# A third pair of weight buffers for the steps, and the product into the state in split parts

## The chip, the cores and the metric

The kernel is written in Bass for one Trainium2 chip and runs on one of its NeuronCores. A core has five engines with queues of their own: TensorE (PE in the profile, with its weight loads as PEld), VectorE (DVE), ScalarE (ACT), GpSimd (POOL) and SyncE (SP), which here only starts transfers. They are ordered by semaphores alone, and each works through its queue in the order of the program. The metric is the device time of one execution in microseconds (us), the median of several runs.

## The reference

One layer of a state-space model on 1,024 tokens of width 512, with a small feed-forward beside it:

```python
xn = layernorm(x)
zxbcdt = xn @ in_proj_w.T                  # gate 8192, x 8192, B 1024, C 1024, dt 128
xBC = silu(causal_conv4(xBC) + conv_b)     # x: 128 heads x 64; B, C: 8 groups x 128
dt = softplus(dt + dt_bias); Adt = -exp(A_log) * dt
# in chunks: y = (C B^T * decay) (dt x)  +  C state * decay  +  D x
#            state = decay * state + B^T (decay * dt x)
y = y * silu(gate)
y = y * rsqrt(mean(y*y over each group of 1024) + eps) * norm_w
attn = y @ out_proj_w.T
# feed-forward: in each block of 32 of the 1,792 inner units only the one with the
# largest value of xn @ c1.T @ c2.T takes part
out = x + attn + (relu(xn @ w1.T) * chosen) @ w2t
```

All inputs and outputs are float32.

## The kernel before, in words

**Split products.** Where a product of float32 numbers is done in F32R, the quicker and coarser matmul form, each operand is kept as a high part (a copy rounded into F32R) and a low part (the number less its high part), and three matmuls, high by high, high by low and low by high, add up in PSUM. ScalarE makes the high part and GpSimd the low part. Products in plain F32 need no parts.

**The steps (`prologue`).** The feed-forward runs in STEPS = 28 steps, 14 slices of 128 inner units for each half of the tokens. Step n has an `inward` product (L764, twelve matmuls of 512 columns: three for each of four slices of the width), a selection mask that VectorE makes in `pick` and TensorE turns in `turn` (L780), the masked hidden units `hm` (`hidden_units`, L595), and an `outward` product (L793, twelve matmuls). Each product takes a weight tile of 128x512 from DRAM, called an item. Item 2n-1 is that of `inward(n)` (`item1`), item 2n+2 that of `outward(n)` (`item2`). An item is loaded by SP into one of AHEAD = 3 raw buffers `wxs` (L298), and `high(i)` on ScalarE (L445) and `low(i)` on GpSimd (L324) split it into one of two pairs `wxp[:, i % 2]`. So the high part of item i waits until the product that used item i-2 is done. TensorE's order is `gate(n+2)`, `inward(n+1)`, `turn(n+1)`, `outward(n)`. In step n ScalarE and GpSimd make the parts of the hidden units (`high_hidden` L462, `low_hidden` L334), then those of item 2n+2, then those of item 2n+3. In steps 12 to 19 the output weights of the first group pass through one tile `stage` as well: SP loads it (L311), ScalarE scales it (L523) and makes its high part (L525), GpSimd makes the low part (L413), SP stores both (L307, L308), and then loads the next. SP's queue holds, in turn, the load of an even item 2n+4, these stores, the load of the odd item 2n+5, and the next load of `stage`. At the end `high_tile` and `low_tile` (L450, L328) split the first two weight tiles of the scan, once the steps' products have freed the two pairs.

**The scan (`scan`).** For each half of the tokens and each of 8 groups (16 units), 18 weight tiles are projected onto 512 tokens (`project`, L1147): 8 x tiles, B and C, which are convolved (VectorE, `convolve`, L1626) and go through Silu into `xT`, and 8 z tiles, which go through Silu into `gT`. A unit has 4 cells of 128 tokens, so there are 64 cells; cell q does the scan of its tokens, while the tiles of the next unit are projected in between, 4 or 5 in a cell. The last unit has none. TensorE's order in cell q is: two tiles, the products within the chunk (`diagonal`, L1205), exponents of the decay (`segment`, L1212), a tile, the product out of the state (`from_state`, L1167), a tile, `segment`, the gram product (`gram`, L1236 and L1237), the output projection of cell q (`project_out`: high by high L1260, high by low weights L1246, low by high L1267; in the first cell of a unit L1267 comes before L1246), `square_sum` (L1276), a fifth tile if there is one, the product into the state (`into_state`, L1180: two plain F32 matmuls of 512 columns, for 56 of the 64 cells), and `turn_x` (L1192), transposes for the cell after the next.

Around it, on VectorE: `scale_x` writes `xdt` (L1711) and `xdec` (L1714), `add_state` (L1662) and `scale_state` (L1644) keep the state S, `take_gram` writes `gb` (L1721), `add_diagonal` and `gate` write y over the gate values `gT` (L1678, L1702), `sum_tiles` adds the squares of the eight tiles of y (L1737), reading with a step of 128 elements, `add_out` adds to `acc` (L1750). On ScalarE: `leave_bank` takes a projected tile out of PSUM (`tap` L1383, or `gate` L1391) and makes the high part of the tile after the next (L1376), `high_y` makes the high part of y (L1441), `square` its squares (L1434), `exp_a` and `exp_b` the decays (L1414, L1418). On GpSimd: the low part of each tile (L1526), `low_y` the low part of y (`yl`, L1557), `join` (L1550) and `rnorm` (L1574).

## Time and profile before

| what | value |
|---|---|
| runs | 1936.75, 1937.0 and 1935.7 us, median 1936.75 us |
| the profiled execution | 1943.26 us, its span 1941.5 us |
| mean granted TensorE clock in it | 0.988 of full speed |
| PE, matmuls | 1866.8 us busy, 96% of the span |
| PEld, weight loads | 1466.4 us, 76% |
| DVE | 1456.4 us, 75% |
| ACT | 1171.3 us, 60% |
| POOL | 956.3 us, 49% |
| DMA | 264.6 MB, mean 136 GB/s |

The steps with what precedes them last until about 263 us, the scan fills the rest. A row of the order of time gives the start, the duration, the engine, the line, the operation with the tiles written and read, and how many records are merged in it; in brackets, how long the engine was idle before it, and what released it. Records of TensorE overlap their neighbours, so that its pace is read from start to start. A plain F32 matmul leaves two records.

### The profile page before, as it was taken

Reading aid. Unit: us, or ns where it says so; the run is one execution under the profiler, and the core shown is the slowest. Engines: PE = TensorE matmul, PEld = TensorE weight load, DVE = VectorE, ACT = ScalarE, POOL = GpSimd, SP = SyncE. Lnnn points to the kernel's source line nnn. Section 1 sums busy time; section 2 is a strip of 40 time slices with the busy share of each in tenths; the row PEclk is TensorE's granted clock in tenths of the full one; section 3 lists DMA queues with packets and bytes.
Section 4 is the critical chain, followed back from the end, with each engine's and each line's share of the span. In section 5 each row is a group of like instructions: output and inputs, shape, how many; then the busy total and the mean of one; then the engine's idle time right before and its main releaser. Section 6 shows DMA issues by size and latency. Waiting matters only on the chain.

```text
span 1941.5 us, 29126 instructions
## 1 busy us (share of the span) xinstructions
PE 1866.8 (96%) x10310; PEld 1466.4 (76%) x10310; DVE 1456.4 (75%) x1713; ACT 1171.3 (60%) x1910; POOL 956.3 (49%) x704
## 2 busy tenths in 40 slices
PE   6897899999999999999999999999999999999987
PEld 5675667777777777777777777878787878787865
DVE  7976645878787877878786878686877787777766
ACT  4334346767777676767676556566665666565643
POOL 4765753545555455555454444444444444444333
PEclk9999999999999999999999999999999999999998
DMA  3324463445464646464647353333424252424231
GB/s 98 110 86 145 121 220 93 128 159 182 134 207 133 219 136 221 125 209 127 212 134 239 86 166 116 111 113 94 147 77 156 83 161 82 156 72 155 70 122 44
DMA packets 123981, 264.60 MB, mean 136 GB/s; under 512 B 18496, under 2 KB 25408, under 8 KB 123584
## 3 DMA queue, kind: packets, MB, share of 16 engines
q1 hardware_dynamic: 89120, 161.55, 26.6%
q10 hardware_dynamic: 34720, 101.20, 16.4%
q8 instruction: 85, 1.39, 0.3%
q14 instruction: 56, 0.46, 0.1%
HBM read 216.82 MB, written 45.88 MB: 135 GB/s over the span
## 4 chain that ended last, share of the span: by engine, by line
PE 79%; DMA 6%; POOL 5%; DVE 3%; issue 3%; ACT 3%; ACTq 1%; SPq 0%; DVEq 0%; POOLq 0%
PE bank L1147 38%; PE bank L1205 5%; PE bank L1246 5%; PE bank L1267 5%; PE bank L1260 5%; PE bank L1180 5%; PE bank L1167 4%; DMA wosl<-wlo_scratch 3%; PE bank L1212 3%; PE bank L793 3%; PE bank L1192 3%; POOL wxp L324 2%; DMA wlo_scratch<-stage 1%; POOL hmp L334 1%; PE bank L764 1%
## 5 line engine op out<-in xcount | busy, mean ns | idle before, releaser
L1147 PE MATMUL bank<-xnp,wxp 128*128 128x512 f32 x3432 | 863.3, 404 | 8.3 <-POOL wxp L1526 3.6
L1147 PEld LDWEIGHTS bank<-xnp,wxp 128*128 128x128 f32 x3432 | 635.6, 189 | 160.1 <-POOL wxp L1526 11.4
L1526 POOL TENSOR_TENSOR wxp<-wxs,wxp 128x512 fp32r<-128x512 f32 x286 | 382.1, 1339 | 530.7 <-ACT wxp L1376 530.0
L1626 DVE SCALAR_TENSOR_TENSOR conv<-bank,cws,conv 128x509 f32<-128x509 f32 (+2 forms) x480 | 358.0, 746 | 11.3
L1383 ACT ACTIVATE conv<-bank,cbs,cws 128x512 f32<-128x512 f32 x160 | 124.1, 776 | 281.5 <-PE bank L1147 258.1
L1557 POOL TENSOR_TENSOR yl<-gT,yh 128x1024 fp32r<-128x1024 f32 x63 | 153.6, 2438 | 216.3 <-ACT yh L1441 216.3
L1729 DVE SCALAR_TENSOR_TENSOR M<-M,gb 128x1024 f32<-128x1024 f32 x128 | 174.1, 1361 | 7.5 <-DVE gb L1721 0.5
L1376 ACT ACTIVATE wxp<-wxs 128x512 fp32r<-128x512 f32 x286 | 178.1, 623 | 0.0
L1427 ACT ACTIVATE ya<-xT,dch 128x128 f32<-128x128 f32 x512 | 156.2, 392 | 0.0
L1418 ACT ACTIVATE M<-bank 128x1024 f32<-128x1024 f32 x64 | 65.6, 1024 | 133.4 <-PE bank L1212 133.4
L1260 PE MATMUL bank<-wosh,yh 128*128 128x512 f32 x512 | 136.2, 408 | 5.3 <-issue 5.0
L1550 POOL TENSOR_TENSOR ya<-ya,ecs 128x1024 f32<-128x1024 f32 x56 | 134.0, 2392 | 8.5 <-ACT ya L1427 8.5
L1205 PEld LDWEIGHTS bank<-M,xdt 128*64 128x64 f32 x2048 | 113.0, 139 | 27.8 <-issue 25.8
L1205 PE MATMUL bank<-M,xdt 128*64 128x128 f32 x2048 | 128.6, 279 | 5.4 <-DVE acc L1750 3.5
L1246 PE MATMUL bank<-wosl,yh 128*128 128x512 f32 x512 | 132.7, 400 | 0.8 <-DMA wosl<-wlo_scratch 0.7
L1737 DVE TENSOR_REDUCE ys<-xdt 128x128 f32<-128x1024 f32 x64 | 129.4, 2022 | 1.6 <-ACT xdt L1434 1.6
L1267 PE MATMUL bank<-wosh,yl 128*128 128x512 f32 x512 | 130.0, 396 | 0.2 <-POOL yl L1557 0.2
L793 PE MATMUL bank<-wxp,hmp 128*128 128x512 f32 x336 | 96.9, 443 | 32.9 <-POOL wxp L324 30.7
L1672 DVE TENSOR_TENSOR ecs<-bank,ecs 128x1024 f32<-128x1024 f32 x56 | 68.6, 1225 | 76.4 <-PE bank L1167 63.4
L1391 ACT ACTIVATE gT<-bank 128x512 f32<-128x512 f32 x128 | 76.5, 598 | 70.0 <-PE bank L1147 69.3
L1246 PEld LDWEIGHTS bank<-wosl,yh 128*128 128x128 f32 x512 | 96.7, 190 | 26.2 <-DMA wosl<-wlo_scratch 3.2
L1267 PEld LDWEIGHTS bank<-wosh,yl 128*128 128x128 f32 x512 | 96.0, 188 | 24.1 <-POOL yl L1557 0.9
(179 smaller groups left out, 2840.9 us busy)
## 6 DMA issues: line engine op xcount, KB each, us to landing
wxs<-wp SPq DMA_DIRECT2D x288, 256.0 KB, 2.8
wosh<-whi_scratch ACTq DMA_DIRECT2D x64, 512.0 KB, 6.0
wosl<-wlo_scratch ACTq DMA_DIRECT2D x64, 512.0 KB, 11.1
ecs<-ecs_scratch ACTq DMA_DIRECT2D x112, 256.0 KB, 4.5
stage<-wout SPq DMA_DIRECT2D x64, 256.0 KB, 2.9
whi_scratch<-stagh SPq DMA_DIRECT2D x64, 256.0 KB, 2.0
wlo_scratch<-stage SPq DMA_DIRECT2D x64, 256.0 KB, 2.3
wxs<-w SPq DMA_DIRECT2D x56, 256.0 KB, 2.8
```

The costliest lines, as they stand in the source:

```text
L793: last = pe.matmul(total(half * CH + c), hmp[:, n % 2, a, c * P:(c + 1) * P], flat[b], start=f == 0 and a + b == 0, stop=f == FT - 1 and a ...
L1147: last = pe.matmul(bank(k), wxp[:, k % 2, a, kk, :], xnp[:, b, kk, :], start=kk == 0 and a + b == 0, stop=kk == KT - 1 and a == 1)
L1205: last = pe.matmul(Y[part, h // 2 * P:(h // 2 + 1) * P], xdt[:, q % 2, h * HD:(h + 1) * HD], M[:, h, :], start=True, stop=True)
L1246: last = pe.matmul(y_out, yh[:, t, :], wosl[:, t, :], start=False, stop=c == 0 and t == XT - 1)
L1260: pe.matmul(y_out, yh[:, t, :], wosh[:, t, :], start=t == 0, stop=False)
L1267: last = pe.matmul(y_out, yl[:, t, :], wosh[:, t, :], start=False, stop=c > 0 and t == XT - 1)
L1376: act.activation(wxp[:, k % 2, 0], wxs[:, k % AHEAD], ACT.Copy).then_inc(w_hi, 1)
L1427: last = act.activation(ya[:, t, :], xT[u % 2][:, 2 + t, tokens(q)], ACT.Copy, scale=dch[:, g, t:t + 1])
L1526: pool.tensor_tensor(wxp[:, k % 2, 1], wxs[:, k % AHEAD], wxp[:, k % 2, 0], ALU.subtract).then_inc(w_lo, 1)
L1557: pool.tensor_tensor(yl[:], gT[u % 2][:, :, tokens(q)], yh[:], ALU.subtract).then_inc(y_lo, 1)
L1626: last = dve.scalar_tensor_tensor(out=conv[:, n % CB, back:], in0=bank(k)[:, 0:TH - back], scalar=cws[:, g, j, i:i + 1], in1=conv[:, n % C ...
L1729: last = dve.scalar_tensor_tensor(out=M[:, hs], in0=M[:, hs], scalar=1.0, in1=bc(gb[:, 0, :], 1, [P, HG // 2, P]), op0=ALU.min, op1=ALU.mult)
```

## The change

In the steps, split items get buffers of their own, `wfp`, in RING = 3 pairs, and `wxp` is left to the scan. The high part of item i waits for the product that used item i-3. `high(2)` and `low(2)` are done before the first step, and in step n the parts of items 2n+3 and 2n+4 are made after those of the hidden units, in place of 2n+2 and 2n+3. The first two tiles of the scan are split in the last two steps.

In the scan, `into_state` becomes six F32R matmuls in place of two in F32. Its operands get parts: ScalarE copies `xdec` into `xdech` (`high_x`) and `gb[:, 1]` into `gbh` (`high_b`), VectorE subtracts for `xdecl` (`low_x`), GpSimd for `gbl` (`low_b`). A low part lies at the address of what it is taken from (`twice`). The low part of y is in the same way written over `gT`, no longer into a tile `yl`, so that `low_y` waits for the Square of the same cell (`y_sq`) and not for the output projection before. The squares are written with the tile's number innermost, so that the reduction reads neighbours, and their sum lies in the first 128 columns of the same buffer. `high_x(q+1)` stands behind the departure of the first tile of cell q, `high_b(q+1)` behind `exp_b(q+1)`, `low_x(q+1)` behind `gate(q)`, `low_b(q+1)` behind `low_y(q)`.

```diff
--- before
+++ after
@@ -58,6 +58,7 @@
 AHEAD = 3
+RING = 3
...
@@ -321,7 +323,8 @@
                 pool.wait_ge(s_hi, i + 1)
-                pool.tensor_tensor(wxp[:, i % 2, 1], wxs[:, i % AHEAD], wxp[:, i % 2, 0], ALU.subtract).then_inc(s_lo, 1)
+                pool.tensor_tensor(wfp[:, i % RING, 1], wxs[:, i % AHEAD], wfp[:, i % RING, 0],
+                                   ALU.subtract).then_inc(s_lo, 1)
...
@@ -395,14 +399,12 @@
             for n in range(STEPS):
-                if n < STEPS - 1:
-                    low_hidden(n)
-                    low(item2(n))
-                else:
-                    low(item2(n))
-                    low_hidden(n)
-                if n + 2 < STEPS:
-                    low(item1(n + 2))
+                low_hidden(n)
+                for i in (2 * n + 3, 2 * n + 4):
+                    if i < 2 * STEPS:
+                        low(i)
+                if n >= STEPS - 2:
+                    low_tile(n - STEPS + 2)
                 mask_part(n)
...
@@ -505,17 +505,17 @@
             copy_mask(0)
+            high(2)
             for n in range(STEPS):
-                if n < STEPS - 1:
-                    high_hidden(n)
-                    high(item2(n))
-                else:
-                    high(item2(n))
-                    high_hidden(n)
+                high_hidden(n)
+                if 2 * n + 3 < 2 * STEPS:
+                    high(2 * n + 3)
                 if n + 1 < STEPS:
                     copy_mask(n + 1)
-                if n + 2 < STEPS:
-                    high(item1(n + 2))
+                if 2 * n + 4 < 2 * STEPS:
+                    high(2 * n + 4)
+                if n >= STEPS - 2:
+                    high_tile(n - STEPS + 2)
                 if OUTW <= n < OUTW + XT:
@@ -562,8 +562,6 @@
                                       tabs[:, half].rearrange("p g a c h -> p g (a c h)")).then_inc(d_saved, 16)
-            for k in range(2):
-                high_tile(k)
...
@@ -787,7 +785,7 @@
                     pe.wait_ge(s_add, CH)
-                flat = [wxp[:, i % 2, b].rearrange("p k c -> p (k c)") for b in range(2)]
+                flat = [wfp[:, i % RING, b].rearrange("p k c -> p (k c)") for b in range(2)]
                 for c in range(CH):
@@ -907,9 +905,15 @@
+    def twice(name, shape):
+
+        with ExitStack() as once:
+            full = sb(once, name, shape)
+        return full, sb(ctx, name + "l", shape, F32R)
+
     with ExitStack() as ctx:
         xT = [sb(ctx, f"xT{p}", [P, WT, TH]) for p in range(2)]
-        gT = [sb(ctx, f"gT{p}", [P, XT, TH]) for p in range(2)]
+        gT, gTl = zip(*(twice(f"gT{p}", [P, XT, TH]) for p in range(2)))
         wosh = sb(ctx, "wosh", [P, XT, HID], F32R)
@@ -919,13 +923,13 @@
         xdt = sb(ctx, "xdt", [P, 2, GC])
-        xdec = sb(ctx, "xdec", [P, GC])
+        xdec, xdecl = twice("xdec", [P, GC])
+        xdech = sb(ctx, "xdech", [P, GC], F32R)
         ecs = sb(ctx, "ecs", [P, XT, P])
         yh = sb(ctx, "yh", [P, XT, P], F32R)
-        yl = sb(ctx, "yl", [P, XT, P], F32R)
         ya = sb(ctx, "ya", [P, XT, P])
-        ys = sb(ctx, "ys", [P, P])
-        gb = sb(ctx, "gb", [P, 2, P])
+        gb, gbl = twice("gb", [P, 2, P])
+        gbh = sb(ctx, "gbh", [P, P], F32R)
         one = sb(ctx, "one", [P, 1])
...
@@ -999,7 +1004,15 @@
-            return xdt[:, q % 2].rearrange("p (t i) -> p t i", t=XT)
+            return xdt[:, q % 2].rearrange("p (i t) -> p t i", t=XT)
+
+        def square_sums(q):
+
+            return xdt[:, q % 2, 0:P]
+
+        def gated_low(q):
+
+            return gTl[q // CH % 2][:, :, tokens(q)]
@@ -1173,12 +1186,14 @@
                     return
-                pe.wait_ge(x_dec, done(q + 1))
-                pe.wait_ge(g_cp, done(q + 1))
+                pe.wait_ge(x_lo, done(q + 1))
+                pe.wait_ge(b_lo, done(q + 1))
                 pe.wait_ge(e_b, done(q + 1))
                 for b in range(2):
-                    last = pe.matmul(X[:, b * 512:(b + 1) * 512], gb[:, 1, :], xdec[:, b * 512:(b + 1) * 512],
-                                     start=True, stop=True)
+                    part = slice(b * 512, (b + 1) * 512)
+                    pe.matmul(X[:, part], gbh[:], xdech[:, part], start=True, stop=False)
+                    pe.matmul(X[:, part], gbh[:], xdecl[:, part], start=False, stop=False)
+                    last = pe.matmul(X[:, part], gbl[:, 1], xdech[:, part], start=False, stop=True)
                 last.then_inc(st_mm, 1)
...
@@ -1444,6 +1459,20 @@
                         act.activation(yh[:, part], gT[u % 2][:, part, tokens(q)], ACT.Copy).then_inc(y_hi, 1)
+
+            def high_x(q):
+                if dead(q):
+                    act.sem_inc(x_hi, 1)
+                    return
+                act.wait_ge(x_dec, done(q + 1))
+                act.activation(xdech[:], xdec[:], ACT.Copy).then_inc(x_hi, 1)
+
+            def high_b(q):
+                if dead(q):
+                    act.sem_inc(b_hi, 1)
+                    return
+                act.wait_ge(g_cp, done(q + 1))
+                act.activation(gbh[:], gb[:, 1], ACT.Copy).then_inc(b_hi, 1)
...
@@ -1477,6 +1509,8 @@
                     load_ecs(q + 1)
+                if more:
+                    high_x(q + 1)
                 if fill:
@@ -1494,6 +1528,7 @@
                     exp_b(q + 1)
+                    high_b(q + 1)
                 load_row(q + 2)
...
@@ -1551,16 +1586,23 @@
                 u, _, _, _ = place(q)
-                pool.wait_ge(o_mm, done(q))
+                pool.wait_ge(y_sq, done(q + 1))
                 if q + 1 < CELLS:
                     pool.wait_ge(y_hi, done(q + 1))
-                    pool.tensor_tensor(yl[:], gT[u % 2][:, :, tokens(q)], yh[:], ALU.subtract).then_inc(y_lo, 1)
+                    pool.tensor_tensor(gated_low(q), gT[u % 2][:, :, tokens(q)], yh[:], ALU.subtract).then_inc(y_lo, 1)
                 else:
                     for n in range(2):
                         part = slice(n * XT // 2, (n + 1) * XT // 2)
                         pool.wait_ge(y_hi, done(q + 1 + n))
-                        pool.tensor_tensor(yl[:, part], gT[u % 2][:, part, tokens(q)], yh[:, part],
+                        pool.tensor_tensor(gated_low(q)[:, part], gT[u % 2][:, part, tokens(q)], yh[:, part],
                                            ALU.subtract).then_inc(y_lo, 1)
+
+            def low_b(q):
+                if dead(q):
+                    pool.sem_inc(b_lo, 1)
+                    return
+                pool.wait_ge(b_hi, done(q + 1))
+                pool.tensor_tensor(gbl[:, 1], gb[:, 1], gbh[:], ALU.subtract).then_inc(b_lo, 1)
...
@@ -1588,6 +1631,8 @@
                 low_y(q)
+                if q + 1 < CELLS:
+                    low_b(q + 1)
                 for k in tiles_of(q)[3 if closes(q) else 2:4]:
...
@@ -1714,6 +1760,13 @@
+            def low_x(q):
+                if dead(q):
+                    dve.sem_inc(x_lo, 1)
+                    return
+                dve.wait_ge(x_hi, done(q + 1))
+                dve.tensor_tensor(xdecl[:], xdec[:], xdech[:], ALU.subtract).then_inc(x_lo, 1)
+
             def take_gram(q):
@@ -1734,7 +1787,7 @@
                 dve.wait_ge(q_mm, done(q))
-                dve.tensor_reduce(ys[:], squares(q).rearrange("p t i -> p i t"), AX.X, ALU.add).then_inc(y_s, 1)
+                dve.tensor_reduce(square_sums(q), squares(q).rearrange("p t i -> p i t"), AX.X, ALU.add).then_inc(y_s, 1)
...
@@ -1767,6 +1822,8 @@
                 gate(q)
+                if more:
+                    low_x(q + 1)
                 for k in ks[2:3]:
```

## Rows read from the trace of the kernel before

**Rows 1.** Table by stage: us, busy times of five engines, clock, DMA share, GB/s.
```profile
70.00:84.00 14.00, 13.10 (x67) 9.76 (x67) 13.72 (x16) 4.38 (x8) 12.12 (x10) 1.00 0.31 92
182.00:196.00 14.00, 10.20 (x44) 7.90 (x43) 8.46 (x15) 7.74 (x14) 5.27 (x5) 0.76 0.47 151
600.00:1000.00 400.00, 398.12 (x2201) 311.11 (x2200) 309.80 (x350) 281.96 (x463) 212.66 (x164) 1.00 0.53 171
```

**Rows 2.** List of waits in the steps (40 to 275 us): total us, times, longest us.
```profile
PE bank L793 <- POOL wxp L324: 30.7, 21, 3.9
```

**Rows 3.** Order of time, TensorE in the steps: start us, us, engine, line, tiles.
```profile
50.68 4.49 PE L793 MATMUL bank<-wxp,hmp 128*128 128x512 f32 x12 [3.24 <-POOL wxp L324]
...
103.42 3.05 PE L793 MATMUL bank<-wxp,hmp 128*128 128x512 f32 x12
...
110.04 3.06 PE L793 MATMUL bank<-wxp,hmp 128*128 128x512 f32 x12
...
231.44 4.37 PE L793 MATMUL bank<-wxp,hmp 128*128 128x512 f32 x12 [1.76 <-POOL wxp L324]
```

**Rows 4.** Order of time, one step with a wait, GpSimd and TensorE.
```profile
211.71 1.46 POOL L324 TENSOR_TENSOR wxp<-wxs,wxp 128x512 fp32r<-128x512 f32 x1
...
213.21 3.07 PE L793 MATMUL bank<-wxp,hmp 128*128 128x512 f32 x12 [0.49 <-POOL wxp L324]
```

**Rows 5.** Order of time, a turn of the staging tile, SP and ScalarE.
```profile
147.60 0.45 SPq L298 DMA_DIRECT2D wxs<-w  x1
...
149.69 0.33 SPq L311 DMA_DIRECT2D stage<-wout  x1
...
150.66 0.63 ACT L445 ACTIVATE wxp<-wxs 128x512 fp32r<-128x512 f32 x1 [2.81 <-DMA wxs<-w]
...
152.85 0.72 ACT L523 ACTIVATE stage<-stage,nws 128x512 f32<-128x512 f32 x1 [1.55 <-DMA stage<-wout]
...
158.54 0.33 SPq L311 DMA_DIRECT2D stage<-wout  x1
```

**Rows 6.** Order of time, TensorE around the product into the state.
```profile
1016.01 2.03 PE L1267 MATMUL bank<-wosh,yl 128*128 128x512 f32 x8
1017.88 0.28 PE L1276 MATMUL bank<-one,ys 128*128 128x1 f32 x2
1018.02 1.96 PE L1180 MATMUL bank<-xdec,gb 128*128 128x512 f32 x4
1019.82 1.04 PE L1192 MATMUL bank<-ident,xT 128*128 128x128 f32 x8
```

**Rows 7.** Order of time in the first cell of a group, three engines.
```profile
957.24 2.40 POOL L1557 TENSOR_TENSOR yl<-gT,yh 128x1024 fp32r<-128x1024 f32 x1 [2.48 <-ACT yh L1441]
...
958.14 2.58 DVE L1644 TENSOR_TENSOR S<-S,tab 128x1024 f32<-128x1024 f32 x1
...
959.96 2.11 PE L1260 MATMUL bank<-wosh,yh 128*128 128x512 f32 x8
...
961.91 2.03 PE L1267 MATMUL bank<-wosh,yl 128*128 128x512 f32 x8
```

**Rows 8.** Groups by line: busy us, mean ns | idle us before, releaser.
```profile
L1737 DVE TENSOR_REDUCE ys<-xdt 128x128 f32<-128x1024 f32 x64 | 129.4, 2022 | 1.6 <-ACT xdt L1434 1.6
...
L1702 DVE TENSOR_TENSOR gT<-ya,gT 128x1024 f32<-128x1024 f32 x63 | 82.5, 1309 | 3.3
...
L1434 ACT ACTIVATE xdt<-gT 128x1024 f32<-128x1024 f32 x64 | 66.8, 1044 | 0.0
```

**Rows 9.** Order of time in one cell: ScalarE, VectorE, GpSimd.
```profile
1001.86 0.78 ACT L1383 ACTIVATE conv<-bank,cbs,cws 128x512 f32<-128x512 f32 x1 [1.51 <-PE bank L1147]
...
1012.15 1.02 ACT L1418 ACTIVATE M<-bank 128x1024 f32<-128x1024 f32 x1 [2.60 <-PE bank L1212]
1012.48 0.42 DVE L1721 TENSOR_TENSOR gb<-bank,upper 128x256 f32<-128x256 f32 x1 [0.26 <-PE bank L1237]
...
1015.68 1.30 POOL L1526 TENSOR_TENSOR wxp<-wxs,wxp 128x512 fp32r<-128x512 f32 x1 [4.54 <-ACT wxp L1376]
```

40 lines of the change are left out of this document (24 added, 16 removed).

## The prediction

> **What bounds the kernel now.** I read the table by stage first. In the scan TensorE is busy for 398.1 of 400 us and VectorE, the next one, for 309.8 [rows 1]. So in the scan each microsecond of TensorE work is a microsecond of the kernel, and work added to another engine is free as long as it lands in that engine's gaps. In the steps the list of waits shows another picture: TensorE waits 30.7 us, 21 times, ahead of the outward matmuls (L793), always for a GpSimd subtraction at L324 [rows 2]. The order of time shows what such a wait costs besides itself. Two neighbouring steps without one are 6.62 us apart (103.42 to 110.04), their twelve matmuls taking 3.05 us. After long waits the same twelve take longer, in seven steps in all: 4.49 us in the first of them, at 50.68, and 4.37 us in the last, at 231.44 [rows 3]. In such stretches the granted clock is down, to a mean of 0.76 in the worst [rows 1]. It is the lower of two levels (1.2 of 2.4 GHz) for part of the run, after an idle TensorE. Each of the seven loses some 1.4 us by it.
>
> **The change, first part: the steps.** In step n the matmuls at L793 need the low part of the hidden units and of item 2n+2, and GpSimd makes them in this order. The row of such a step: the second subtraction runs from 211.71 for 1.46 us, and TensorE, idle for 0.49 us, starts at 213.21 [rows 4]. With a third home, item 2n+2 is split one step earlier, and TensorE waits for 211.71 at the latest. So a wait shrinks by up to 1.46 us, and where it was long enough to lower the clock, some 1.4 us more come back (4.49 and 4.37 against 3.05, [rows 3]).
>
> I price three stretches.
> (a) Up to step 12 there are three long waits: steps 1, 7 and 10. Three times 1.46, and the clock for two of them (in step 1 more than half of its wait stays, so I leave its clock low), is 4.4 + 2.8 = 7.2 us. The short waits between steps 2 and 6 I count at nothing: VectorE is busy for 13.72 of 14 us there [rows 1] and would set the pace without them.
> (b) Steps 13 to 19 also bring the first group's output weights through one staging tile, and this has a loop of its own in SP's queue. A load of it is issued at 149.69, ScalarE scales it at 152.85, GpSimd subtracts, SP stores both parts, waits for them, and issues the next load at 158.54: 8.85 us a turn, more than the 6.62 us of a step [rows 3, 5]. In the changed order ScalarE has to split item 2n+4 ahead of this scaling. That tile's load is issued right behind the staging load, some 0.4 us later, and a tile issued at 147.60 is taken up at 150.66, 3.06 us on [rows 5]. So scaling starts 0.4 + 3.06 + 0.5 = 3.97 us after the issue, not 3.16, and a turn takes 9.66 us. Six turns lose 4.9 us. At the end of the stretch the subtraction (1.46 us) and one clock loss (1.4 us) are saved: together -2 us. The bounds are -8 (a turn of 10.2 us, and nothing else) and +5 (the turn is not stretched, as the tile's load may land earlier than I have it).
> (c) From step 21 on only GpSimd is late, in all seven steps: 0.49 us in the first [rows 4], 1.76 us in the one at 231.44 [rows 3]. The seven waits, each counted up to 1.46, add up to 6.0 us, and two slowed runs give 1.4 each: 8.8 us.
> Together 7.2 - 2 + 8.8 = 14.0 us; at the best 7.2 + 5 + 8.8 = 21, at the worst, with no clock won back either, 4.4 - 8 + 6.0 = 2. Splitting the scan's first two tiles inside the last steps gives nothing more: their matmuls follow the steps without a gap already.
>
> **Second part: the product into the state.** Its two plain F32 matmuls of 512 columns are four records, from 1018.02 to the next operation at 1019.82: 1.80 us. The new form is six matmuls in F32R. Such matmuls in a row run 0.234 us apart (eight from 1016.01 to 1017.88, [rows 6]) to 0.244 us apart (eight from 959.96 to 961.91, [rows 7]). Six are 1.40 to 1.46 us; I take 1.43, as both rows are of the same shape. That is 0.37 us a cell, and 56 of the 64 cells have the product: 20.7 us, between 19 and 22. The Trainium skill (FP8 and Floating Point Precision, TensorE Precision Notes) says that true FP32 takes four passes through the array and the reduced form reads the same four bytes cut short; with eight passes against six an estimate from it would be a quarter of 1.80, 0.45 us a cell and 25 us. No run so far shows the new form in this place.
>
> What the split adds: a copy of 128x1024 on ScalarE (1.04 us as the Square of this size at L1434), one of 128x128 (under 0.6 us, less than any 512-wide one), a 128x128 subtraction on GpSimd (above nothing, below the 1.30 us of a 128x512 one), and a 128x1024 subtraction on VectorE (1.31 us as at L1702) [rows 8, 9]. VectorE gets something back: the reduction at L1737 takes 2.02 us now, reading with a long step; it will read neighbours, so about as fast as other 1024-wide operations, 1.3 us. Net +0.6 us a cell for VectorE. Per cell of 25 us it has over 5 us free [rows 1]. Where each lands: the first copy goes behind the first tile's departure, ahead of a ScalarE operation that was idle for 1.51 us [rows 9], so it fits. The second copy waits for VectorE's gram product, done at 1012.90, and ScalarE's own exponential is done at 1013.17 [rows 9]: it fits, or costs ScalarE a microsecond. Behind it stand the z tile's Silu, the next tile's high part, and GpSimd's low part, ended at 1016.98 where TensorE wants it past 1020.6, after the eight transposes that begin at 1019.82 [rows 6, 9]: 3.6 us of cover. VectorE's subtraction stands where it waits for TensorE next.
>
> What is no longer covered: the low part of y is now written over gT, so GpSimd may start only after ScalarE's Square, 1.04 us later [rows 8]. In a group's first cell its result is wanted directly behind the first eight output matmuls. There it ended at 957.24 + 2.40 = 959.64, wanted at 961.91: 2.27 us of cover [rows 7]. Of this 1.04 go, and another microsecond may, because this subtraction and VectorE's scaling of the state (L1644) keep each other out: 2.58 us in this row, for an operation of the size of L1702's [rows 8]. The Trainium skill (SBUF, Who interferes with whom) has this as a rule: a VectorE instruction with two SBUF inputs and a GpSimd one that reads SBUF block each other for their whole length; by it the new subtraction joins these. The trace agrees, with that 2.58 us. So cover in 16 cells falls to nearly nothing. I take 3 us lost there, and 1 us elsewhere in the scan, bounds 0 and 12. The last cells, with no tiles to hide anything, gain 0.7 us from the short reduction and lose about as much.
>
> **The sum.** Scan 20.7 - 4 = 16.7; steps 14.0; together 30.7 us. The profiled execution took 1943.3 us around a span of 1941.5, the median of the runs is 1936.75. I take the 30.7 us off the median: 1906.0 us, with a span near 1911.
>
> **Rivals.** (1) The staging loop decides: its turns grow to over 10 us, since a tile's load directly behind the staging load may land later, and clock losses stay. The steps bring 2 us, the whole 19: 1918 us. For it: SP waited in all of these turns; against: only seven steps are concerned. Chance 0.17.
> (2) The thin covers of the scan give way: y's low part late by half a microsecond in 16 cells and VectorE late in a few others, 12 us in place of 4: 1914 us. A slower Square would do this too, as it now writes every eighth element: at the worst 2.02 us as the reduction with its long step had, a microsecond later for GpSimd. The Trainium skill (SBUF, Door 1) has a penalty for each access that leaves a 16-byte line, which both would pay; no row shows a ScalarE write of this kind. Chance 0.15.
> (3) The staging loop is not stretched, 21 us from the steps, and the scan loses nothing: 42 us, 1895 us. For it: ScalarE is idle around the loop's operations. Chance 0.12.
> (4) The change doesn't do what it says: six F32R matmuls with six weight loads take 0.30 us each in this place, the same 1.80 us, and 4 us are lost: 1927 us. Nothing in the rows speaks for it. Chance 0.05.
> (5) Slower: ScalarE's queue is held at the second copy by a late gram product, which VectorE reaches only after the scaling of the state. It decides once the product comes over 3.6 us later than now in every cell; each microsecond beyond costs 60 us over the 60 cells with tiles, so beyond about 4.1 us later the gain is eaten, and at 4.3 us the time is 1948. VectorE's additions ahead of it are 1.3 us plus 1.2 us of exclusion, and part of that runs in idle time, so chance 0.03.
> (6) Losses of (1), (4) and (2) together, nothing left: 1935 us, 0.03.
>
> **Chances and range.** My forecast has 0.45 and its own range 1898 to 1914. From 1894 to 1921 lie it, (1), (2) and most of (3): 0.8 and a little more. What a measurement here can tell from no change is about 0.2%, 3.9 us. Faster 0.94, the same 0.03, slower 0.03.
>
> **What would show it.** In the profile after: the product's six records within 1.43 us; TensorE's waits before the outward matmuls for the hidden units' low part, no longer for the weights', with at most three slowed runs outside steps 13 to 19; staging loads 9.7 us apart; the reduction near 1.3 us; short waits of TensorE for y's low part in first cells. Wrong would be the forecast if TensorE's share in the scan fell under 98%, or if the steps ended as late as now.

## The result and the profile after

The changed kernel takes 1945.9 us (median of 6 runs, 1942.6 to 1952.56), the kernel before took 1937.64 us in the same rounds (6 runs, 1935.7 to 1941.95). The ratio is 1.0042, with a 95% interval of 1.0027 to 1.0056: slower, by 0.4%. I had forecast 1906 us, a range of 1894 to 1921, and a chance of 0.94 that it would be faster. The miss is 40 us on the time, or 39 us if the forecast gain of 30.7 us is set against the measured loss of 8.3.

The profiled execution is the fastest run of the changed kernel (1942.6 us, span 1940.9), while the one of before lay above its median. So the two traces end together, and the 8 us between the medians are not between them. Where the traces differ is still plain to see, because the gains and losses in them are several times as large. I first read what was forecast. These are TensorE's records around the product into the state in an ordinary cell, to be set beside [rows 6]:

```profile
1015.98 1.99 PE L1282 MATMUL bank<-wosh,gT0l 128*128 128x512 f32 x8
1017.80 0.28 PE L1291 MATMUL bank<-one,xdt 128*128 128x1 f32 x2
1017.94 0.48 PE L1194 MATMUL bank<-xdech,gbh 128*128 128x512 f32 x1
...
1019.19 0.40 PE L1196 MATMUL bank<-xdech,gbl 128*128 128x512 f32 x1
1019.42 1.03 PE L1207 MATMUL bank<-ident,xT 128*128 128x128 f32 x8
```

Six matmuls take 1019.42 - 1017.94 = 1.48 us, where four records took 1.80. The whole interval between two cells shrank by 0.36 us wherever nothing else got in the way. That was the 0.37 of the forecast. The groups of instructions by line show the other engines (busy us, mean ns, idle us before and what ended it), beside [rows 8]:

```profile
L1782 DVE SCALAR_TENSOR_TENSOR M<-M,gb 128x1024 f32<-128x1024 f32 x128 | 212.1, 1657 | 7.1
L1449 ACT ACTIVATE xdt<-gT 128x1024 f32<-128x1024 f32 x64 | 143.8, 2246 | 0.0
...
L1592 POOL TENSOR_TENSOR gT1l<-gT,yh 128x1024 fp32r<-128x1024 f32 x31 | 78.3, 2525 | 176.2 <-ACT xdt L1449 176.2
L1605 POOL TENSOR_TENSOR gbl<-gb,gbh 128x128 fp32r<-128x128 f32 x56 | 78.2, 1396 | 16.7 <-ACT gbh L1475 16.5
...
L1790 DVE TENSOR_REDUCE xdt<-xdt 128x128 f32<-128x1024 f32 x64 | 77.3, 1208 | 2.8 <-ACT xdt L1449 2.8
L1768 DVE TENSOR_TENSOR xdecl<-xdec,xdech 128x1024 fp32r<-128x1024 f32 x56 | 77.2, 1379 | 5.6 <-ACT xdech L1468 5.6
```

The reduction fell from 2022 to 1208 ns, but the Square, which writes every eighth element now, rose from 1044 to 2246 ns. I had bounded it at 2.02 us. GpSimd's low part of y waits for it throughout. GpSimd's 128x128 subtraction for B takes 1.40 us, above my bound of 1.30. The list of TensorE's waits in the scan (325 to 1880 us; before, the line of y's low part had none there):

```profile
PE bank L1282 <- POOL gT1l L1592: 6.2, 5, 2.7
PE bank L1160 <- POOL wxp L1561: 4.4, 12, 1.2
PE bank L1282 <- POOL gT0l L1592: 4.1, 5, 1.4
```

The longest of these, in order of time. The Square starts at 1065.25, GpSimd can start at 1067.53, TensorE starts at 1070.23 after 2.66 us of idle time:

```profile
1065.25 2.20 ACT L1449 ACTIVATE xdt<-gT 128x1024 f32<-128x1024 f32 x1
...
1067.53 2.64 POOL L1592 TENSOR_TENSOR gT1l<-gT,yh 128x1024 fp32r<-128x1024 f32 x1 [6.35 <-ACT xdt L1449]
1070.13 1.44 POOL L1605 TENSOR_TENSOR gbl<-gb,gbh 128x128 fp32r<-128x128 f32 x1
...
1070.23 2.11 PE L1282 MATMUL bank<-wosh,gT1l 128*128 128x512 f32 x8 [2.66 <-POOL gT1l L1592]
```

The table by stage says it in one row. TensorE is busy for 394.0 of 400 us where it was 398.1 [rows 1], ScalarE for 315.5 where it was 282.0:

```profile
600.00:1000.00 400.00, 394.03 (x2232) 316.29 (x2231) 323.34 (x364) 315.47 (x494) 236.87 (x182) 1.00 0.52 171
```

There is also a wait that I hadn't seen at all. B's high part of the first cell can only be copied after the gram product, and GpSimd's subtraction follows at 315.95, behind a tile's low part that keeps GpSimd busy until then. TensorE has nothing else to do meanwhile, and after 4.42 us of it (0.56 before) its eight transposes take 1.91 us, not 1.04, as at the lower of its two clocks:

```profile
317.48 0.47 PE L1194 MATMUL bank<-xdech,gbh 128*128 128x512 f32 x1 [4.42 <-issue]
...
319.50 1.91 PE L1207 MATMUL bank<-ident,xT 128*128 128x128 f32 x8
```

**A measure that is finer than the time.** The timed runs of one kernel spread over some 8 us, and most of the differences here are smaller. But the scan's cells repeat closely. I took the start of each cell's first diagonal matmul (L1205 before, L1220 after) from the order of time, and compared each interval from cell to cell with the same interval of before. In undisturbed cells two traces agree within 0.03 us. The table gives the sums of the differences in us, over eight cells of a kind in the first half and seven in the second, with the last group by itself. "1st" is the interval that begins with a group's first cell. The first row is what the product alone should give: 0.36 us in each of the 55 intervals that hold one (in the second half the 3rd intervals hold none).

```
                      first half               second half              last    cell 0
kernel              1st    2nd    3rd    4th    1st    2nd    3rd    4th   group  to 63
forecast, product  -2.9   -2.9   -2.9   -2.9   -2.5   -2.5    0.0   -2.5   -0.7  -19.8
after               7.8    3.2   -2.9   -2.1   -0.3   -2.5   -0.2    0.2    1.6    4.7
scan_alone          9.5    4.3   -2.8   -0.7   -1.6   -2.5   -0.2    0.2    2.4    8.6
square_rows16       3.1   11.0   -2.9    1.4   -2.0   -2.5   -0.2   -2.5    1.9    7.3
steps_alone         0.5    0.5    0.0    2.7   -0.1    0.0    0.0    0.0    0.0    3.6
strided_in_before  -0.8    0.0    0.0    0.2   -0.1    0.0    0.0    0.0   -3.0   -3.7
steps_and_strided  -1.4   -1.2    0.0   -0.3   -0.1    0.0    0.0    0.0   -2.5   -5.5
wait_in_before     -0.9   -0.2    0.0    2.4   -0.1    0.0    0.0    0.0   -1.0    0.3
wait_and_strided    5.7   -0.9    0.0    1.1    2.4    0.0    0.0    0.2    2.9   11.4
square_of_high     -0.2   10.9   -2.9   -2.1   -2.7    0.6   -0.2   -2.5   -3.7   -2.9
no_low_b           -3.2    9.4   -2.8    0.3   -2.7    0.8   -0.3   -2.5   -2.7   -3.7
no_split_x         -4.1    3.4   -2.9    0.2   -2.7   -1.9   -0.3   -2.5   -4.4  -15.1
high_and_rows16     1.7   11.0   -2.8   -2.2   -2.7    1.3   -0.3   -2.5    0.6    4.1
b_after_tile        2.5    3.7   -2.9   -2.7   -2.7   -1.8   -0.2   -2.5    0.2   -6.6
b_after_strided     0.4    4.6   -3.0   -2.2   -2.7   -1.8   -0.2   -2.6   -2.9  -10.4
x_low_later        12.6    4.2   -1.4   -1.9    0.7    1.4   -0.2   -2.5   -3.2    9.6
first_b_on_vector   2.9    3.0   -2.8   -1.9   -2.7   -1.8   -0.2   -2.5   -2.7   -8.8
```

The row of the changed kernel: the 3rd cells gain what they should, and the first half's 1st and 2nd cells, the second half's 1st and 4th, and the last group give all of it back. The scan should gain 19.8 and loses 4.7, so 24.5 us are lost between cell 0 and cell 63, and 3.6 more before cell 0 (the scan's first tile starts 7.7 us sooner than before, cell 0 only 4.1). I had allowed 4 us for both.

The first half's 4th cells also hold the load of the tokens' other half (xnp), whose wait differs by up to 2.7 us between two runs of anything. No reading rests on that column, though the last column of the table has it in. How far the other columns can be trusted is told by pairs of kernels with the same scan: before and steps_alone, after and scan_alone, strided_in_before and steps_and_strided. Within such a pair a column differs by up to 1.7 us and the total by 1.8 to 3.9 us, so smaller differences show nothing.

### The profile page after: what moved, and what is told of

The parts are those of the page before. It is cut to its first block, busy times and chain, and to the rows that moved or that the text cites. A ratio compares the mean times of both kernels' runs of the same rounds, so it can differ in the third digit from the quotient of the medians.

```text
span 1940.9 us, 29607 instructions
## 1 busy us (share of the span) xinstructions
PE 1847.9 (95%) x10422; PEld 1483.3 (76%) x10422; DVE 1476.0 (76%) x1769; ACT 1309.4 (67%) x2022; POOL 1038.6 (54%) x760
## 4 chain that ended last, share of the span: by engine, by line
PE 50%; DVE 11%; ACT 11%; POOL 9%; DMA 8%; issue 8%; ACTq 2%; SPq 1%; DVEq 0%; POOLq 0%
PE bank L1160 25%; DMA wlo_scratch<-stage 4%; PE bank L1220 4%; PE bank L1180 4%; PE bank L1282 3%; PE bank L1261 3%; DVE conv L1672 2%; PE bank L1275 2%; DMA stage<-wout 2%; PE bank L1227 2%; ACT xdt L1449 2%; PE bank L1207 2%; POOL stage L1610 2%; DVE S L1690 2%; POOL wxp L1561 1%
## 5 line engine op out<-in xcount | busy, mean ns | idle before, releaser
L1782 DVE SCALAR_TENSOR_TENSOR M<-M,gb 128x1024 f32<-128x1024 f32 x128 | 212.1, 1657 | 7.1
L1592 POOL TENSOR_TENSOR gT1l<-gT,yh 128x1024 fp32r<-128x1024 f32 x31 | 78.3, 2525 | 176.2 <-ACT xdt L1449 176.2
L1592 POOL TENSOR_TENSOR gT0l<-gT,yh 128x1024 fp32r<-128x1024 f32 x32 | 80.3, 2510 | 161.1 <-ACT xdt L1449 161.1
L1449 ACT ACTIVATE xdt<-gT 128x1024 f32<-128x1024 f32 x64 | 143.8, 2246 | 0.0
L1220 PEld LDWEIGHTS bank<-M,xdt 128*64 128x64 f32 x2048 | 110.6, 137 | 26.2 <-issue 26.2
L1220 PE MATMUL bank<-M,xdt 128*64 128x128 f32 x2048 | 125.9, 276 | 3.8 <-DVE acc L1803 3.5
L791 PE MATMUL bank<-wfp,hmp 128*128 128x512 f32 x336 | 93.8, 434 | 27.3 <-POOL hmp L337 26.4
L1180 PEld LDWEIGHTS bank<-xT,S 128*128 128x128 f32 x896 | 108.5, 192 | 6.7 <-issue 1.7
L1180 PE MATMUL bank<-xT,S 128*128 128x128 f32 x896 | 109.1, 275 | 0.7 <-DVE xdec L1760 0.7
L1275 PEld LDWEIGHTS bank<-wosh,yh 128*128 128x128 f32 x512 | 91.6, 189 | 23.7 <-issue 6.4
L326 POOL TENSOR_TENSOR wfp<-wxs,wfp 128x512 fp32r<-128x512 f32 x56 | 80.3, 1442 | 53.4 <-ACT wfp L446 53.3
## 6 DMA issues: line engine op xcount, KB each, us to landing
wosl<-wlo_scratch ACTq DMA_DIRECT2D x64, 512.0 KB, 11.2
```

Source lines behind the costliest of these rows:

```text
L1180: last = pe.matmul(Z[:, t * P:(t + 1) * P], S[:, t * P:(t + 1) * P], xT[u % 2][:, 1, tokens(q)], start=True, stop=True)
L1220: last = pe.matmul(Y[part, h // 2 * P:(h // 2 + 1) * P], xdt[:, q % 2, h * HD:(h + 1) * HD], M[:, h, :], start=True, stop=True)
L1275: pe.matmul(y_out, yh[:, t, :], wosh[:, t, :], start=t == 0, stop=False)
L1449: act.activation(squares(q), gT[u % 2][:, :, tokens(q)], ACT.Square).then_inc(y_sq, 1)
L1592: pool.tensor_tensor(gated_low(q), gT[u % 2][:, :, tokens(q)], yh[:], ALU.subtract).then_inc(y_lo, 1)
L1782: last = dve.scalar_tensor_tensor(out=M[:, hs], in0=M[:, hs], scalar=1.0, in1=bc(gb[:, 0, :], 1, [P, HG // 2, P]), op0=ALU.min, op1=ALU.mult)
```

## The experiments

Each ratio is to the kernel before, from runs in the same rounds.

**The two parts apart.** steps_alone has the changed steps and the old scan; scan_alone the old steps and the changed scan.

> The steps part alone (three homes), the scan as before. The changed kernel was 8 us slower than before in the timed runs, although its scan begins 7.7 us earlier in the profile. Theory A (the steps gain what the profile shows, the scan loses it twice over): 7 to 9 us below before, 1929 to 1931 us. Rival B (the profile of before is one with slow steps, 6 us above its median, and in an ordinary run the steps gain little): 0 to 3 us below before.

> The product into the state from split parts, with the Square in its new layout, y's low part in place and the two new splits; the steps as before. Theory A: the scan alone loses 15 to 17 us against before, 1953 us, since 8 us of the steps' gain are missing. Rival B: it loses 8 to 10 us, 1946 us, as much as the whole change did.

steps_alone: 0.9987 (0.9974 to 0.9999). scan_alone: 1.0081 (1.0066 to 1.0096), 15.7 us slower by the medians. So the scan loses nearly as much as it was to win, the 15 to 17 us of theory A. By size the steps lie between the two theories: 2.6 us by the medians of steps_alone, 7.5 us as the difference of scan_alone and the changed kernel (1.0081 and 1.0042). That they gain at all is plainer in the traces than in the first of these. There the scan's first tile starts at 265.8 to 267.5 us in the five with the old steps and at 257.7 to 264.0 in the fifteen with the new ones.

**The Square's write, and GpSimd's wait for it.** The first edit gives the changed kernel a Square that writes neighbours, as 16-bit numbers to make room for the sums; the second gives the kernel before the strided Square; the third and fourth add the wait.

```diff
 square_rows16 (from the changed kernel)
-            return xdt[:, q % 2].rearrange("p (i t) -> p t i", t=XT)
+            return xdt[:, q % 2, 0:GC // 2].bitcast(BF16).rearrange("p (t i) -> p t i", t=XT)
-            return xdt[:, q % 2, 0:P]
+            return xdt[:, q % 2, GC // 2:GC // 2 + P]
 strided_in_before (from before), and wait_and_strided
-            return xdt[:, q % 2].rearrange("p (t i) -> p t i", t=XT)
+            return xdt[:, q % 2].rearrange("p (i t) -> p t i", t=XT)
 wait_in_before (from before), and wait_and_strided
                 pool.wait_ge(o_mm, done(q))
+                pool.wait_ge(y_sq, done(q + 1))
```

> The changed kernel with one thing other: the squares are written tile after tile as before (neighbours, but as 16-bit numbers, so that they leave room for the sums behind them), and the reduction reads with the long step again. Theory C (the strided write of the Square, 2.25 us for 1.04, is what eats the scan's gain: GpSimd's low part of y waits for it and ScalarE's queue is behind it): Square back to 1.04 us, TensorE's waits ahead of the output's low matmuls gone but for some tenths, and 15 us or more below the changed kernel, 1931 us or less. Rival D (the wait for the Square itself costs, however short the Square is, or the copy and subtraction of the group's B do): Square at 1.04 us but less than 5 us below the changed kernel, 1941 us or more.

> The kernel before with nothing changed but the layout of the squares: the Square writes every eighth element and the reduction reads neighbours. GpSimd doesn't wait for the Square here. Theory C: the Square takes 2.25 us and the reduction 1.2 us here too; what hangs on ScalarE alone (its 1.2 us more a cell) shows as 0 to 4 us more than before, and the rest of the loss needs GpSimd's wait. Rival E (ScalarE's load is the loss): 10 us or more above before.

> The kernel before with one wait more: GpSimd's subtraction for y's low part waits for the Square too (1.04 us long here), into a buffer of its own as before. Theory F (the scan loses by this wait in the groups' first cells and in the last unit): visible waits of TensorE ahead of the output's low matmuls of some 2 to 4 us in sum, and 2 to 5 us more than before. Rival G (the wait is harmless, the loss comes from the two new splits and their places): no more than before, within 0.1%.

> The kernel before with the same wait and the strided Square (2.25 us) with the short reduction. Theory F: waits ahead of the output's low matmuls as in the changed kernel, 8 to 11 us in sum, and 8 us or more over before; with it, all but the new splits is accounted for. Rival G: within 3 us of before, as the short reduction gave back 4 us.

square_rows16: 1.0043 (1.0029 to 1.0058), no better than the changed kernel. Theory C fell as it was put, and rival D's number came: the Square came back to 1.04 us, the first half's 1st cells went from 7.8 to 3.1 and the second half's 4th to the full -2.5, but the first half's 2nd cells went from 3.2 to 11.0. Something else stood ready there. The edit changes two things at once, since the reduction is back at 2.02 us as well: TensorE now waited for the sums (L1291) 4.1 us, 6 times (325 to 1880 us), where the changed kernel's list had no such line.

strided_in_before: 0.998 (0.9969 to 0.9991). The strided write alone costs the kernel before nothing; the short reduction behind it gives 3 us in the last group. wait_in_before: 0.9982 (0.997 to 0.9995), though the cells are 0.3 us longer in sum than before's. The wait alone costs nothing either. (I have no cause in the trace for that 0.18%, and so take no difference in time under 0.2% between two kernels as shown.) Both together, wait_and_strided: 1.005 (1.0035 to 1.0065), 11.4 us over before in the trace, 15.1 over strided_in_before. Its waits ahead of the output's low matmuls:

```profile
PE bank L1267 <- POOL yl L1558: 5.0, 8, 2.2
```

That is the same place as in the changed kernel (2.66 us in the worst cell there), without any split product. In the first cell of [rows 7] the cover was 2.27 us, and that row was of one cell. Before the change twelve of the sixteen first cells had 2.1 to 2.9 us of it, three had 0.05 to 0.65, and the last group's had none. One of the three, in the trace of before:

```profile
1063.54 2.39 POOL L1557 TENSOR_TENSOR yl<-gT,yh 128x1024 fp32r<-128x1024 f32 x1 [4.28 <-ACT yh L1441]
...
1066.55 2.03 PE L1267 MATMUL bank<-wosh,yl 128*128 128x512 f32 x8
```

With the wait and a Square of 1.04 us (wait_in_before), the low part was still in time in fifteen of the sixteen. With one of 2.25 us (wait_and_strided) GpSimd's subtraction, which takes 2.4 to 3.1 us there, was late in thirteen. So the wait and the stride cost nothing one by one and 15 us together. TensorE's waits for y's low part, the last group's with them, are 9 of these 15 us; the other 6 are not traced to a wait.

**Squares of two bytes, and B's low part on VectorE.**

> The changed kernel with the squares as 16-bit numbers in the changed kernel's order, so that the Square's step is 16 bytes and not 32, and the reduction reads neighbours. If the step in bytes sets the price of the Square: it comes back to 1.04 to 1.3 us with the reduction at 1.2 us or less, both sides of the swap won; TensorE's waits in first cells fall under 5 us in sum, and the kernel is 8 us or more below the changed one, near 1936. If each element costs its write, whatever the step: 2.25 us as in the changed kernel, and its time, 1946.

> As the run before it (16-bit squares), and B's low part (128x128) is made by VectorE ahead of its second multiplication of the mask, not by GpSimd. Theory H (GpSimd's 1.4 us for it, behind y's low part, is what makes the next tile's low part late, 4.4 us of waits ahead of the projections, and costs 3.6 us ahead of the first cell): these waits fall to under 1 us, the first cell begins 3 us sooner, 4 to 7 us below the run before it. Rival: the wait for the copy only moves to VectorE, same time within 2 us.

squares16_near: 1.0537 (1.0517 to 1.0556), 103 us slower. The groups by line:

```profile
L1449 ACT ACTIVATE xdt<-gT 128x1024 bf16<-128x1024 f32 x64 | 309.6, 4837 | 0.0
...
L1790 DVE TENSOR_REDUCE xdt<-xdt 128x128 f32<-128x1024 bf16 x64 | 77.7, 1214 | 22.9 <-ACT xdt L1449 22.6
```

The smaller step made the Square not faster but twice as slow, 4837 ns; both expectations were wrong. b_on_vector stands on it and gave 1.063 (1.0609 to 1.0651). With TensorE waiting 65 us for y's low part behind this Square in the one, the pair says nothing on B's low part; that was a poor choice of ground.

**The wait taken away with its cause.** The Square reads y's high part, which stays where it is, so GpSimd may write over y at once.

```diff
-                act.activation(squares(q), gT[u % 2][:, :, tokens(q)], ACT.Square).then_inc(y_sq, 1)
+                act.wait_ge(y_hi, done(q + 1 if q + 1 < CELLS else q + 2))
+                act.activation(squares(q), yh[:], ACT.Square).then_inc(y_sq, 1)
...
-                pool.wait_ge(y_sq, done(q + 1))
```

> The changed kernel, but the Square reads y's high part and not y itself, so that GpSimd needn't wait for the Square before it writes y's low part in place (the norm's sum of squares is then of y rounded to its high part). Theory F (this wait, together with the Square's 2.2 us, is half of what the scan lost): visible waits ahead of the output's low matmuls back to under 1 us in sum, second-half groups' first cells 0.36 us shorter than before instead of as long, the last group 2 to 3 us shorter than in the changed kernel; 8 to 10 us below the changed kernel, 1936 to 1938 us. Rival (the low part is late since GpSimd and ScalarE are full): under 3 us below it.

1.0018 (1.0007 to 1.0029), 4.6 us below the changed kernel by the ratios, so between the two expectations. (The two were not run in the same rounds.) In the cells it did what theory F says: 1st cells of the first half 7.8 to -0.2, of the second half -0.3 to -2.7, the last group 1.6 to -3.7. But again the 2nd cells of the first half rose to 10.9. Here is such a cell in order of time, ScalarE, GpSimd and TensorE:

```profile
568.55 2.33 ACT L1450 ACTIVATE xdt<-yh 128x1024 f32<-128x1024 f32 x1
...
570.57 1.17 ACT L1433 ACTIVATE M<-bank 128x1024 f32<-128x1024 f32 x1
571.56 0.38 ACT L1476 ACTIVATE gbh<-gb 128x128 fp32r<-128x128 f32 x1
571.96 1.28 ACT L1406 ACT_TABLE_LOAD   x1
573.25 0.60 ACT L1406 ACTIVATE gT<-bank 128x512 f32<-128x512 f32 x1
573.75 0.62 ACT L1391 ACTIVATE wxp<-wxs 128x512 fp32r<-128x512 f32 x1
...
572.02 0.46 POOL L1605 TENSOR_TENSOR gbl<-gb,gbh 128x128 fp32r<-128x128 f32 x1 [1.03 <-ACT gbh L1476]
574.45 1.27 POOL L1562 TENSOR_TENSOR wxp<-wxs,wxp 128x512 fp32r<-128x512 f32 x1 [1.97 <-ACT wxp L1391]
...
575.77 3.08 PE L1160 MATMUL bank<-xnp,wxp 128*128 128x512 f32 x12 [1.01 <-POOL wxp L1562]
```

TensorE waits for the next tile's low part. GpSimd waited 1.97 us for its high part, and ScalarE made this behind the Square, the exponential, the copy of B and a table load. The list of ScalarE's waits in square_of_high (340 to 1880 us) shows that this copy also stops the queue, because VectorE's gram product is not there yet (total us, times, longest us):

```profile
ACT gbh L1476 <- DVE gb L1774: 14.0, 23, 0.7
```

**Which of the operations in front of the tile.** no_low_b leaves out GpSimd's subtraction for B (its place keeps the wait), no_split_x leaves out the copy and the subtraction for x, both from square_of_high. steps_and_strided joins the two things that had gained by themselves.

> As square_of_high, but B's low part is left out: GpSimd's subtraction of 128x128 (1.4 us) isn't made and the third pair of matmuls reads B's high part in its place. Theory H (GpSimd's subtraction makes the next tile's low part late, and the first cell's product): the 4.4 us ahead of the first cell shrink to 2.9, waits for the tiles' low parts fall from some 4 us to under 1, together 4 to 6 us below square_of_high. Rival: it lies in GpSimd's gaps, within 2 us of it but for the first cell.

> As square_of_high, but the split of the decayed x is left out: VectorE writes it in F32R at once, ScalarE's copy (1.06 us) and VectorE's subtraction (1.38 us) aren't made, and the second pair of matmuls reads the high part again. If the load of these two on the engines is what stretches the first two cells of the first half's groups (some 12 us over the sum of the product's gain there): the first half's cells all gain 0.3 us or more, 8 to 12 us below square_of_high. Rival (the split of x is free, as the prediction had it): within 2 us of it.

> What gained by itself: the three homes in the steps, and the strided Square with the short reduction in the scan of before (no split product, y's low part in its own buffer). If the two gains add (0.13% and 0.20%): 6 us below before, ratio 0.9967. If they are noise or overlap: within 2 us of before.

no_low_b: 0.9978 (0.9966 to 0.999). Its 2nd cells stay at 9.4, so GpSimd's subtraction isn't the tile's delay. Its gain lies ahead of cell 0, where TensorE's wait falls from 4.42 to 0.91 us. The table by stage, TensorE alone, has the granted clock behind it, first in square_of_high and then in no_low_b:

```profile
317.00:323.00 6.00, 5.89 (x19) 0.53 0.58 167
```

```profile
317.00:323.00 6.00, 6.00 (x39) 1.00 0.72 176
```

So there are 63.7 us from the scan's first tile to cell 0, as before the change (331.21 - 267.47), against 69.8 in square_of_high. no_split_x: 0.9962 (0.9948 to 0.9976), 10.8 us below square_of_high; 12.2 in the cells. The prediction had this split at no cost. steps_and_strided: 0.9968 (0.9958 to 0.9978). The product of the two ratios, 0.9967, was expected, as it is if the two gains add.

**The Square's length, or the order.** high_and_rows16 is square_of_high with the Square and the sums of square_rows16, so 1.04 us long again. square_after_tile puts the strided Square behind the third tile's departure, and TensorE's sum behind the fifth tile. b_after_tile is high_and_rows16 with B's split moved:

```diff
                 if more:
                     exp_b(q + 1)
-                    high_b(q + 1)
...
                     for k in ks[2:3]:
                         leave_bank(k)
+                if more:
+                    high_b(q + 1)
...
+                for k in [] if closes(q) else tiles_of(q)[2:3]:
+                    low(k + 2)
                 if q + 1 < CELLS:
                     low_b(q + 1)
-                for k in tiles_of(q)[3 if closes(q) else 2:4]:
+                for k in tiles_of(q)[3:4]:
                     low(k + 2)
...
-            into_state(0)
             turn_x(1)
+            into_state(0)
```

> The Square reads y's high part (so that GpSimd doesn't wait for it) and writes neighbours, as 16-bit numbers: 1.04 us on ScalarE, and the reduction's 2.0 us on VectorE. If the Square's length on ScalarE, ahead of the next tile's high part, is what stretches the first half's second cells (+10.9 us over eight cells): these fall to about 0 or below, and the time to 8 to 12 us under square_of_high, 1926 to 1929 at before 1935. If VectorE's longer reduction takes over (TensorE waits for the sums, as in square_rows16): no more than 4 us under it.

> As square_of_high (strided Square of 2.3 us), but in cells with tiles the Square stands behind the third tile's departure on ScalarE, and TensorE sums the squares behind the fifth tile. ScalarE's chain to the third tile's low part is 2.3 us shorter, so TensorE's waits of 0.2 to 1.0 us at 17 us into the first half's second cells vanish; the ones at 26 us (0.8 us each) may stay. 4 to 8 us under square_of_high; if the sums come late in place of them, same within 2 us.

> As high_and_rows16, and the copy of B (ScalarE) and its low part (GpSimd) stand behind the third tile, with the transposes of the second cell's x ahead of the first cell's product. If these two hold the tile up: 2 to 5 us under high_and_rows16, the first cell 1 us earlier. If B's split is late for the product instead (it stands 3 us behind where it stood): waits ahead of L1194's matmuls, same or slower.

high_and_rows16: 1.0028 (1.0015 to 1.004), 2nd cells 11.0. My guess that the Square's length stretches them fell: 1.2 us off it changed nothing there. The list of ScalarE's waits (340 to 1880 us) shows why. The wait at the copy of B grew from 14.0 us to

```profile
ACT gbh L1476 <- DVE gb L1774: 24.6, 24, 1.9
```

In the first half's 2nd cells ScalarE starts this copy 13.1 us into the cell in both kernels, for VectorE's gram product ends 12.8 us into it in square_of_high and 13.1 here (means of eight). So ScalarE reached the copy earlier and waited there. The reduction on VectorE is 0.8 us longer in this kernel, so the two effects are not fully apart.

b_after_tile: 0.9991 (0.9978 to 1.0003); 2nd cells 11.0 to 3.7 in the first half, 1.3 to -1.8 in the second. So it is the place of B's split. The edit moves both of its operations, and no_low_b has shown that GpSimd's isn't the one that delays the tile, so this points to ScalarE's copy. square_after_tile: 1.0543 (1.0523 to 1.0563). VectorE's queue comes to the reduction before the Square is made and stops there; TensorE's first wait in its list:

```profile
PE bank L1291 <- DVE xdt L1795: 40.0, 28, 3.4
```

**The order, with the strided Square.** b_after_strided is square_of_high with the edit above; x_low_later also moves VectorE's subtraction for x behind the reduction; first_b_on_vector instead gives VectorE the first cell's subtraction for B, ahead of its first weighing.

> square_of_high (strided Square of y's high part, short reduction) with the copy of B and its low part behind the third tile and the second cell's transposes ahead of the first cell's product. By b_after_tile the first half's second cells fall by 7 us and the second half's by 3: 10 us under square_of_high, ratio to before 0.997, the first half's first cells at about 0 over eight. If ScalarE's longer Square undoes it: under 5 us below square_of_high, 0.9995 or more.

> As b_after_strided, and VectorE's subtraction for x's low part stands behind the reduction, where VectorE was idle for 2.4 us waiting for ScalarE's part of a tile, and no longer behind the gating, ahead of the third tile's convolution and the scaling of the state. If this subtraction is what still holds the first half back (leaving the split of x out gave 10.8 us): the first two cells gain 3 to 8 us more over the half, and the kernel is the fastest, ratio 0.993 to 0.995, under steps_and_strided's 0.9968. If it comes late for the product there: waits ahead of the product's second pair of matmuls, no gain or a loss.

> As b_after_strided, with one subtraction moved: B's low part of the first cell alone is made by VectorE, ahead of its first weighing of the mask, and not by GpSimd beside it (1.4 us there, and 2.5 us of TensorE's waiting left). If the two engines' exclusion holds the first product up: the wait ahead of it falls to under 1 us as in no_low_b, TensorE keeps its clock through the next ten us, the first cell begins 3 to 5 us sooner after the scan's first tile, and the ratio to before is about 0.993 to 0.995. If not: 0.9957 as b_after_strided.

b_after_strided: 0.9957 (0.9941 to 0.9973). It is the fastest kernel by its ratio, faster than both kernels. It has the whole change with the Square reading y's high part and B's split behind the third tile. But its interval overlaps those of no_split_x and steps_and_strided, and the last of these has no split product at all. From the scan's first tile to cell 63 the two traces take 1648.8 us (b_after_strided) and 1648.0 us (steps_and_strided), which is the same by this measure. So no run here shows that the split product, even in its best order, is worth more than the steps and the short reduction without it. ScalarE's wait for the gram product is gone from its list but for one of 0.7 us, and GpSimd's subtraction for B, away from VectorE's weighing, takes a third of what it took in the changed kernel (508 ns for 1396; 1105 in square_of_high):

```profile
ACT gbh L1476 <- DVE gb L1777: 0.7, 1, 0.7
```

```profile
L1606 POOL TENSOR_TENSOR gbl<-gb,gbh 128x128 fp32r<-128x128 f32 x56 | 28.4, 508 | 6.2 <-ACT gbh L1476 6.2
```

x_low_later: 1.0059 (1.0041 to 1.0078), the second of its expectations. The 1st cells rise to 12.6, with TensorE waiting for that subtraction ahead of the product and for the output weights. first_b_on_vector: 0.9969 (0.9956 to 0.9982). TensorE no longer waits ahead of the first product (2.54 us of it were left in b_after_strided), and cell 0 begins 64.4 us after the scan's first tile instead of 68.0. The mechanism was right, but the ratio isn't below b_after_strided's; the intervals overlap, and 3.6 us is about what this measurement can't tell.

## Why the prediction was wrong, by its steps

**The product: right.** 1.48 us for 1.43, 0.36 us a cell for 0.37. The estimate of 0.45 from the Trainium skill's four passes (FP8 and Floating Point Precision, TensorE Precision Notes) does not hold for these rows.

**The losses in the scan: the step that failed.** The prediction had "3 us lost there, and 1 us elsewhere in the scan, bounds 0 and 12". The trace has 24.5 us between the cells and 3.6 ahead of them. Neither of my two signs of a wrong forecast showed it: TensorE was still busy for 98.5% of the scan from cell 0 to 1873 us (99.6% before), above the 98% that I had set, and the steps ended earlier. Three things went into it:

- *The Square at 1.04 us.* I took the length of the contiguous write from [rows 8] and kept the strided one for a rival, bounded by the reduction at 2.02 us. It takes 2.25, which leaves nothing of the 2.27 us of cover in [rows 7], and I had read that cover from one cell for all sixteen. wait_in_before against wait_and_strided shows what this does: 0.3 us and 11.4 us. The Trainium skill's rule that I set beside the rival (SBUF, Door 1) pointed the right way; I should have put it into the sum, since the edit changes the access pattern of exactly this instruction.
- *"It fits, or costs ScalarE a microsecond"*, of the copy of B. I looked at what is behind it for the product (3.6 us of cover) and left out the tile's high part behind it in the same queue. Moving it behind the tile gives 7.5 us in the cells. This is rival (5), in small: ScalarE's queue held at this copy by the gram product, 6.1 us in all in the changed kernel (9 times, at most 3.0 us) and 14.0 us in square_of_high (23 times, at most 0.7), not in every cell. I had priced it only as one that begins 3.6 us late. And for cell 0, where no tile hides it, I had no term: 3.6 us.
- *The split of x "fits".* Each of its two operations lay in idle time of its own engine in [rows 9], and was counted at nothing. Leaving it out gives 10.8 us. The rows were of a 3rd cell of the first half, and the 3rd cells did gain in full; the loss is in the 1st and 2nd. The staging of the output weights doesn't set these apart, as all four cells stage equally. VectorE's queue does. "VectorE's subtraction stands where it waits for TensorE next" holds in the 3rd cells: the gram product ends 11.2 us into them in before, in square_of_high and in no_split_x alike. In the first half's 2nd cells VectorE comes to the gram product without a wait already in before (0.0 us of idle time ahead of it in all eight), so that the subtraction pushes it back: it ends 11.8 us into the cell in before and in no_split_x, and 12.8 in square_of_high (means of eight). ScalarE's copy of B and the tile's high part follow it. This points at VectorE's subtraction, but no run leaves out one of the two operations alone. I did not find an order that hides it: x_low_later made it worse.

These three do not add up to 28 us by themselves, since each wait hides a part of the next (square_rows16 and square_of_high both moved a loss from the 1st cells to the 2nd). With the first two mended (b_after_strided), 10.4 us stay where the product was to give 19.8, and 2.9 of them are in the last group, where the short reduction alone gave 3.0.

**The steps: right in kind, too large.** TensorE's waits at L791 are for the hidden units' low part, no longer for the weights' (before, 21 waits and 30.7 us [rows 2]):

```profile
PE bank L791 <- POOL hmp L337: 26.4, 15, 3.6
```

In the traces the steps bring 6.1 us (means of the starts of the scan's first tile), by the timed runs 2.5 to 7.5, for 14.0. Stretch (a) came out near, 8.4 us at step 12 for 7.2, but in part by luck: steps 3 to 6, whose short waits I had counted at nothing, brought 2.8 us of it, and step 7, which was to bring 2.9, brought next to nothing, as a new wait of 1.74 us stands in step 8. (b) cost more than its 2 us. The staging turn rose to 9.98 us for the 9.66 forecast (seven loads from 132.37 to 192.27; before, its mean was 9.05, and my 8.85 was one turn). Four of the steps 13 to 19 are slowed, as the one at 172.35, where before it was two; outside them two are left:

```profile
172.35 5.46 PE L791 MATMUL bank<-wfp,hmp 128*128 128x512 f32 x12 [3.62 <-POOL hmp L337]
```

By step 21 only 4.0 us of the 8.4 were left. (c) won 6.3 of 8.8 by step 26 and gave 2.6 back in the last step, to a wait of 2.71 us for the hidden units: GpSimd makes a low part of the scan's first tiles (L331, 1.29 us, new in this place) and a select (L397, 2.00 us) before it comes to theirs. I had written of that move only that it gives nothing more. In the staging stretch there is another wait that I hadn't priced: ScalarE now waits 43.8 us, 15 times, for the loads of the items (11.4 us, 5 times before), 39.1 us of it between 130 and 203 us and 4.64 us of it ahead of the row above. That these loads set the pace of the steps now would be my reading; no run tried it.

**The tail.** Forecast as a gain of 0.7 us that is lost again: the last group lost 1.6 us with the wait for the Square, and gained 2.5 to 4.4 in every kernel with the short reduction and without that wait.

**The chances.** Slower had 0.03, as I saw it only as one large mechanism. It came as several small ones. The slower Square stood in rival (2), the late gram product in rival (5); the split of x and the copy's place ahead of the tile I had found to fit, and the first cell had no term. They were not independent either: the Square and both copies stand in ScalarE's queue, the copy of B there waits for VectorE's, and taking one loss away brought out another (7.8 to 3.1 in one column, 3.2 to 11.0 in the next).
